# Second attention of a four-stage transformer kernel: value groups of 3, 3, 2 and 2 rounds instead of 2, 2, 3 and 3, and another order of a pair's pieces

## What is computed

```python
q = split_heads(x @ Wq + bq)          # 16 heads of 16
k = split_heads(x @ Wk + bk)
v = split_heads(x @ Wv + bv)
attn = jnp.einsum('bhqd,bhkd->bhqk', q, k) / jnp.sqrt(jnp.float32(HEAD_DIM))
alibi = -slopes[:, None, None] * (Tx - 1 - jnp.arange(Tx, dtype=jnp.float32))[None, None, :]
attn = attn + alibi
attn = jnp.where(causal, attn, jnp.finfo(jnp.float32).min)
p = jax.nn.softmax(attn, axis=-1)
out = jnp.einsum('bhqk,bhkd->bhqd', p, v).transpose(0, 2, 1, 3).reshape(Bx, Tx, C)
return out @ Wo + bo
```

## Time and profile before

| | us |
|---|---|
| median of 3 runs | 1660.38 |
| lowest and highest | 1658.6 and 1664.19 |
| the profiled execution, its own time | 1651.18 |
| its span, first to last instruction | 1649.3 |
| second attention, slots 1 to 6 of the first sequence | 571.67 to 671.12 |
| one such slot | 16.57 to 16.58 |
| PE busy in the span | 1560.8 (95%) |
| DVE, ACT, POOL busy | 1093.4, 932.1, 640.5 |

### The profile page before, as it was taken

How to read it: one execution, slowest core, us unless ns; L and a number is a source line. 1 busy time by engine, 2 the same in 40 slices (tenths; PEclk the granted TensorE clock), 3 DMA queues, 4 the chain that set the end, 5 groups by cost and what they waited for, 6 DMA issues and landing times.

```text
span 1649.3 us, 31099 instructions
## 1 busy us (share of the span) xinstructions
PE 1560.8 (95%) x10834; PEld 1349.9 (82%) x10834; DVE 1093.4 (66%) x2693; ACT 932.1 (57%) x2054; POOL 640.5 (39%) x590
## 2 busy tenths in 40 slices
PE   8999999999999999999998999999999999998996
PEld 7888889889888677688888898898988886776885
DVE  6767667676645787574577676766766377874755
ACT  5666565665444577643656655556654346776452
POOL 1635444554561101252535445444554510031631
PEclk9999999999999999999999999999999999999998
DMA  3110000020120432034220100000201113322133
GB/s 132 46 52 17 27 1 16 25 91 1 39 69 11 73 53 57 25 115 144 78 93 8 70 18 26 16 25 0 91 1 58 50 34 61 61 61 98 56 129 106
DMA packets 48195, 88.04 MB, mean 53 GB/s; under 512 B 9600, under 2 KB 30480, under 8 KB 46928
## 3 DMA queue, kind: packets, MB, share of 16 engines
q1 hardware_dynamic: 43552, 75.28, 15.8%
q0 software_dynamic: 3744, 10.26, 1.7%
q10 hardware_dynamic: 768, 0.79, 0.2%
HBM read 60.18 MB, written 19.76 MB: 48 GB/s over the span
## 4 chain that ended last, share of the span: by engine, by line
PE 66%; DVE 14%; ACT 9%; issue 6%; POOL 4%; DMA 1%; ACTq 0%; DVEq 0%; POOLq 0%; SPq 0%
PE ps L408 16%; PE ps L410 14%; PE ps L409 14%; PE ps L1176 4%; PE ps L1193 4%; PE ps L1136 4%; ACT E L1390 3%; DVE nmax L1789 3%; PE ps L899 2%; POOL E L2246 2%; ACT PT_h L1372 2%; DVE PT_l L1764 1%; PE ps L1172 1%; DVE On L1707 1%; PE ps L825 1%
## 5 line engine op out<-in xcount | busy, mean ns | idle before, releaser
L1390 ACT ACTIVATE E<-ps,nmax 128x128 f32<-128x128 f32 (+7 forms) x256 | 188.9, 741 | 207.5 <-DVE nmax L1789 207.0
L2243 POOL TENSOR_SCALAR E<-E,mixc 128x128 f32<-128x128 f32 (+7 forms) x128 | 96.9, 757 | 400.0 <-DVE mixc L1757 400.0
L1789 DVE TENSOR_REDUCE nmax<-ps 128x1 f32<-128x128 f32 (+7 forms) x256 | 183.2, 748 | 12.9 <-PE ps L874 12.7
L1552 ACT ACTIVATE PT<-ps 128x512 f32<-128x512 f32 x288 | 155.0, 601 | 58.9 <-PE ps L1176 57.0
L2246 POOL TENSOR_TENSOR E<-E 128x128 f32<-128x128 f32 (+7 forms) x128 | 182.3, 1424 | 10.7
L408 PE MATMUL ps<-V_h,PT_h 128*128 128x256 f32 x576 | 166.7, 289 | 0.0
L409 PE MATMUL ps<-V_l,PT_h 128*128 128x256 f32 x576 | 162.6, 282 | 0.0
L410 PE MATMUL ps<-V_h,PT_l 128*128 128x256 f32 x576 | 162.6, 282 | 0.0
L408 PE MATMUL ps<-K_h,Q_h 128*128 128x512 f32 (+3 forms) x384 | 147.3, 384 | 8.6 <-ACT E L1390 5.2
L1764 DVE TENSOR_TENSOR PT_l<-ps,PT_h 128x128 fp32r<-128x128 f32 (+7 forms) x128 | 96.7, 755 | 68.2 <-ACT PT_h L1372 67.5
L2005 DVE CUSTOM_DVE_ANT_0 masked<-ps,causal 128x128 bf16<-128x128 f32 (+3 forms) x256 | 111.2, 486 | 41.6 <-PE ps L1136 39.7
(11 more groups left out here) (265 smaller groups left out, 4585.4 us busy)
## 6 DMA issues: line engine op xcount, KB each, us to landing
Wa_raw<-in_wa SPq DMA_DIRECT2D x8, 1024.0 KB, 6.0
Fw_raw<-in_fa SPq DMA_DIRECT2D x32, 256.0 KB, 2.7
E_raw<-in_fe SPq DMA_DIRECT2D x8, 768.0 KB, 7.5
xs<-in_xs SPq DMA_DIRECT2D x2, 2967.0 KB, 12.5
Wo_raw<-in_wo SPq DMA_DIRECT2D x8, 512.0 KB, 3.5
yg<-ys SPq DMA_DIRECT2D x8, 512.0 KB, 5.2
xg<-xs SPq DMA_DIRECT2D x6, 645.0 KB, 7.9
KS<-QK_h SPq DMA_DIRECT2D x56, 64.0 KB
```

The source lines that it names most:

```text
L1390: nc.scalar.activation(e[:, 0:w], ps[m][:, 0:w], ACT.Exp, bias=nmax[:, s % 4, m:m + 1], accum_out=lsum[:, s % 4, m:m + 1]).then_inc(exp_do ...
L1552: nc.scalar.activation(PT[:, at:at + HALF], bank1(RING1 + n % RING1), ACT.Exp, scale=SCALE1).then_inc(t_used, 1)
L1789: nc.vector.tensor_reduce(nmax[:, s % 4, m:m + 1], ps[m][:, 0:(s % NT + 1) * P], AX.X, ALU.max, negate=True).then_inc(nmax_ready[m], 1)
```

## The change

`ROUNDS_V` and the order of the table change; nothing else does. All pieces are the same in kind and number.

```diff
-ROUNDS_V = (2, 2, 3, 3)
+ROUNDS_V = (3, 3, 2, 2)
...
-        order = """a0 a1 a2 t0 t1 t2 a3 w3 c0 a4 t3 t4 a5 t5 a6 a7 t6 o0 a8 t7 a9 a10 t8 t9 v0 a11 m0 t10 a12
-                   a13 v1 t11 t12 a14 t13 a15 t14 n0 a16 a17 t15 v2 m1 t16 t17 n1""".split()
+        order = """a0 t0 a1 t1 t2 a2 t3 a3 t4 a4 t5 w3 a5 t6 a6 c0 t7 a7 t8 t9 a8 o0 a9 t10 t11 a10 a11 v0
+                   a12 a13 t12 t13 a14 a15 v1 m0 t14 a16 t15 a17 t16 m1 n0 t17 v2 n1""".split()
```

## The result

The changed kernel takes 1667.28 us (median of 5 runs, 1666.68 to 1668.81) against 1660.38 for the kernel before in the same comparison (1658.6 to 1664.19). The ratio is 1.0039, 95% interval 1.0027 to 1.0050: slower by 0.4%, 6.5 us by the ratio and 6.9 us between the medians. The forecast was 1666.2.

The account below looks back on a forecast made before the run. The prediction took PE, never idle, to bound the kernel. Steady slots +4.4, first slots +1.5 and last slots -0.1 gave +5.8 to +5.9 us on the median of 1660.38: 1666.2 us, range 1659 to 1672.

Parts of the forecast that it names:

- What bounds the slot: Steady slot: PE is never idle, its pieces take 16.50 us, and waits cost only 0.07 us a slot.
- The group sizes alone, price 0: Value groups: same four sizes in other places, 4.44 us both times; 0.20 extra taken between v2 and n1.
- t3, 0.24 late: Start of a steady slot: t3 waits for t0's exponential, which runs behind n1's casts on ACT; 0.24 us.
- t9 and t11, 0.13 and 0.08: Middle of a steady slot: t9 waits for t6's bank, 0.13 us; t11 for t8's exponential, 0.08 us.
- The end, v2 and n1 just in time: End of a steady slot: v2 and n1 don't wait, with margins of 0.07 and 0.04 us.
- Together 16.95: A steady slot with the three waits: 16.95 us, 0.37 more than now; 12 of them add 4.4 us.
- The first slot, +0.76: Slot 0, twice: less work lies ahead of the late t3, so 17.13 us, +0.76, in all +1.5.
- The last slot, -0.05: Last slot, twice: ACT sets the pace and a shorter w3 pays for a later v0; -0.05, in all -0.1.
- Slot 6: Counted among the 12 steady slots at +0.37 us; POOL's wait for a0 of the last pair priced 0.
- The first (margins open, 0.7 a slot): Rival: small margins on ACT's loop open, 0.7 to 0.8 us a slot, +10 us, 1670.6; chance 0.14.
- The second (no change): Rival: n1's casts don't hold t0 as counted; only +2 us, 1662.4; chance 0.25.
- The third (the gaps behind groups are waits for DVE): Rival: gaps ahead of a11, a4 and a10 are DVE waits the order removes; -4 to -5.5 us, 1655.5; chance 0.13.

Follow-up runs that it names:

- e5: The changed kernel with m0 moved ahead of v0 and n0 ahead of v1; slot 17.33 us against 16.95 expected.
- e2: The changed kernel with w3 moved ahead of t3; 1665.51 us against 1664.41 for the kernel before, ratio 1.0008.
- e8: The changed kernel with c0 moved directly behind w3, ahead of t6; steady slots of 16.85 us, one run.
- e3: The changed kernel with w3 and c0 ahead of t3 and t9 behind a8; 1665.98 us, ratio 1.0011 to the kernel before.
- e4: The changed kernel with GpSimd's weight splitting started by the last a piece of the last pair, not the first; slot 6 took 18.54 us.
- e6: The changed kernel with GpSimd's weight splitting started by the last casts of the last pair; slot 6 took 16.96 us, whole run 1659.43.
- f3: A reordered three-group version (3, 3, 4 rounds) with its middle group cut in two around a16; slots 16.62 to 16.67 us, on average 0.35 more.

## Why the prediction held, point by point

- **What bounds the slot.** Right: 16.50 us of pieces in sequence, of which the kernel before wasted 0.07. The experiments moved the slot by waits or by fixed group prices, and no order with four groups went below the pieces.
- **The group sizes alone, price 0.** Right for their sum: 1.43, 1.22, 1.03 and 0.79 in the changed kernel. The 0.20 between v2 and n1 was too much; e5 gives 0.12.
- **t3, 0.24 late.** Measured 0.26, removed by e2 alone. The hand-over (0.73 from the exponential's end to t3's end) was right to the hundredth, since the wait in slot 0 of the kernel before was the same one.
- **t9 and t11, 0.13 and 0.08.** Measured 0.07 and 0.10, 0.17 instead of 0.21 together. c0 holds t11 (e8), t6's exponential holds t9, as said; w3's place has no part in it. A full piece ends 0.54 behind the exponential here, not 0.59.
- **The end, v2 and n1 just in time.** v2 waits 0.03 and n1 0.05, where margins of 0.07 and 0.04 were given. With 0.12 instead of 0.20 for n1's place, n1 would have ended at 2.36 behind t16 by its pieces; it ends at 2.43. Two small errors cancelled, which was luck: without these waits the slot would be 16.88.
- **Together 16.95.** Measured 16.96, +0.38 for +0.37.
- **The first slot, +0.76.** Measured +0.84 and +0.82.
- **The last slot, -0.05.** Measured -0.16 and -0.17. The value groups next to each other (v2, w3) seem to pay the fixed price once: they take 1.76 together in the chain, where 1.00 + 0.79 are 1.79. A group that had to wait is 0.07 to 0.11 longer there (before: 1.50 for 1.43, 1.33 for 1.22), which leaves 1.65 to 1.69.
- **Slot 6.** The step that was missing. It was priced as a steady slot, +0.37, and came out at +0.74 and +0.75. The text looked for what GpSimd waits for, not for whom it holds up. The new place of m1 is not the reason. In a steady slot m1's last instruction ends at 603.45 in the kernel before and at 621.60 in the changed one. From there to the end of an n1 that waited for it are 0.14 + 0.60, and n1 ended at 604.85 and 622.98, so m1 could be 0.66 and 0.64 later at no cost. What differs is the length of the hold. Before, it was 0.24 and 0.38 (0.41 and 0.55 for 0.17), within that slack; in the changed kernel it is 0.98 and 1.20, beyond it by 0.34 and 0.56, as the slots say. The hold lasts for what is left of GpSimd's subtraction when DVE comes to L2018: before, it had run for 1.4 and 1.3 us of 1.83 by then, now for 0.7 and 0.5. The slack is borne out by other runs: holds of 0.66 (e2), 0.77 (e3) and 1.39 (e8) in the first sequence made slot 6 0.02, 0.14 and 0.74 longer than its neighbours. So 0.9 of the 6.5 us hang on how two engines that don't wait for each other happen to meet; that the new order makes them meet so was not shown. The Trainium skill, SBUF — State Buffer, Who interferes with whom, says that a DVE instruction with two SBUF inputs contends with a GpSimd instruction that reads SBUF, and that DVE in a two-port mode, which a cast can enter, and GpSimd block each other for a whole instruction. e4 agrees for both kinds (the cast at L2021 took 1.83, the two-input L2023 0.73, for 0.17 each), and in e6, with no GpSimd instruction beside them, the holds are gone.
- **The sum.** Expected +5.9: 4.4 + 1.5 - 0.1. Measured in the slots +6.5: 1.9 + 1.75 for slots 1 to 5, 1.5 for the two slots 6, 1.7 for the first and -0.3 for the last. The forecast of its own case, +3.5 to +8, holds, and would hold without the 0.9 of the holds too, at +5.6.
- **The rivals.** The first (margins open, 0.7 a slot) didn't come, though the margins at v2 and n1 were used up and overrun by 0.03 and 0.05. The second (no change) is refuted by the wait at t3, which is there in full. The third (the gaps behind groups are waits for DVE) is refuted by f3, where the same gap stands 1.1 us after DVE was done.

## What to carry to other kernels

When one engine is the bound and never idle, count its pieces first: the sum says how much an order can still win, here 0.07 of 16.57 us, while an order can always lose more. An even mix of two kinds of pieces is no aim in itself; what counts is how much other work lies between a piece and the one that takes its bank again, and that work has to be largest where the consumer has something else to do first (here ACT's casts). Then look for fixed prices that a different grouping avoids (f3's group of strips more cost 0.35 a slot), and for small DVE instructions that a long GpSimd instruction can hold: count the slack between them and the piece that waits for them (0.64 here) against the longest hold (1.83).

## What the hardware showed that I hadn't expected

- DVE instructions on 128 x 8 elements, 0.17 us alone, took 1.15, 1.37 and 1.83 us beside a GpSimd instruction of 1.83 us and ended within 0.03 us of it; a cast with one input (L2021) was held like the instructions with two. The maxima that read PSUM weren't: in slot 6 they take 0.69 us on average (L2009), as in other slots.
- Going to strips of 32 columns and back costs 0.14 + 0.20 us of PE each time (f3), with transposes behind it 0.12 for the 0.20 (e5); two groups in a row (v2, w3 in the last slot, 1.76) seem to pay it once.
- A PE row that waits for a semaphore in the middle of a run is shown as busy, so a stretch with 16.96 us of 16.96 busy held about 0.5 us of waits.
